# A state-space scan and an attention layer in one pipeline: TensorE's order made over two ticks, running sums on VectorE

## What is computed

```python
# layer 0, per image, over L = 4096 positions, 128 inner channels, 16 states
x, z = split(seq @ in_proj_w)
x = silu(conv1d(x, conv1d_w) + conv1d_b)             # 4 taps
dt, B, C = split(x @ x_proj_w)
delta = softplus(dt @ dt_proj_w + dt_proj_b)
h[t] = exp(delta[t] * A) * h[t-1] + (delta[t] * x[t]) * B[t]
y[t] = sum_n h[t] * C[t] + x[t] * D
seq = (y * silu(z)) @ out_proj_w
# layer 1, per image, hw = 4096
out_c = softmax(xc @ xc.T) @ x                       # 64 x 64
energy = q.T @ k                                     # 4096 x 4096
out_s = v @ softmax(energy, axis=-1).T
out = x + w_bn @ concat(out_c, out_s)
```

## Time and profile before

| | before |
|---|---|
| median of 3 runs | 8331.68 us (8329.12 to 8335.33) |
| profiled execution, span | 8332.7 us |
| PE busy | 7638.9 us, 92% |
| DVE busy | 6757.6 us, 81% |
| ACT busy | 5962.3 us, 72% |
| POOL busy | 3408.2 us, 41% |
| largest groups of PE | PV 2192.6 us, dif and max 1588.4 us, S 1567.9 and 1561.7 us, SUM 1071.1 us |
| largest groups of DVE | scan 2293.8 + 312.4 us, DBU 1514.0 us, maximum 1369.6 us |

### The profile page before, as it was taken

One profiled execution on the slowest core, in us unless ns is written; L12 is line 12 of the kernel. 1 busy time (PEld: TensorE's weight loads), 2 busy tenths in 40 slices (PEclk: granted clock), 3 DMA queues, 4 the chain that ended last, 5 costly groups with the idle time before them and its releaser, 6 DMA issues.

```text
span 8332.7 us, 153459 instructions
## 1 busy us (share of the span) xinstructions
PE 7638.9 (92%) x48454; PEld 2320.1 (28%) x48454; DVE 6757.6 (81%) x10982; ACT 5962.3 (72%) x10582; POOL 3408.2 (41%) x4135
## 2 busy tenths in 40 slices
PE   9963489999999999999989999999999999999999
PEld 2311122222222222222222222222222222222322
DVE  2238899898989898998989898998989898989721
ACT  1124578787877787887878787887877787878754
POOL 0016544444444444444444444444444444444300
PEclk9975699999999999999999999999999999999999
DMA  9838877878787878788777878787878878777500
GB/s 153 134 95 216 216 198 199 200 196 203 197 198 198 200 196 203 194 200 204 193 192 191 204 197 200 198 201 196 202 196 200 201 192 207 194 200 200 149 24 11
DMA packets 886525, 1531.01 MB, mean 184 GB/s; under 512 B 409480, under 2 KB 459472, under 8 KB 885712
## 3 DMA queue, kind: packets, MB, share of 16 engines
q1 hardware_dynamic: 882640, 1520.79, 74.8%
q10 hardware_dynamic: 3072, 0.40, 0.0%
HBM read 1326.69 MB, written 176.95 MB: 180 GB/s over the span
## 4 chain that ended last, share of the span: by engine, by line
PE 42%; ACT 3%; issue 2%; DMA 1%; ACTq 1%; DVE 1%; SPq 0%; DVEq 0%
PE bank L915 12%; PE bank L840 6%; PE bank L930 6%; PE bank L903 5%; PE bank L905 5%; PE bank L877 3%; ACT L1011 1%; ACT gains L956 1%; PE bank L885 1%; PE bank L872 1%; PE bank L862 1%; ACT pr L1011 1%; PE bank L858 1%; ACTq L1033 1%; DMA s1kx<-kx_d 1%
## 5 line engine op out<-in xcount | busy, mean ns | idle before, releaser
L1273 POOL TENSOR_TENSOR hst<-hst,cbc 128x512 f32<-128x512 f32 x2048 | 2609.9, 1274 | 3617.7 <-DVE bank L1145 3595.2
L1156 DVE TENSOR_TENSOR_SCAN hst<-dA,carry,bank 128x512 f32<-128x512 f32 x1792 | 2293.8, 1280 | 95.7 <-ACT dA L1017 23.7
L1011 ACT ACTIVATE pr<-bank 128x512 f32<-128x512 f32 x4096 | 2226.7, 603 | 59.4 <-PE bank L905 57.7
L915 PE MATMUL bank<-pr,vt 128*32 128x512 f32 x16384 | 2192.6, 607 | 0.0
L956 ACT ACTIVATE gains<-bank 128x512 f32<-128x512 f32 x2048 | 1224.2, 598 | 1106.1 <-PE bank L840 707.2
L1017 ACT ACTIVATE dA<-lanes,small 128x512 f32<-128x512 f32 x2048 | 1502.1, 733 | 349.8 <-DMA lanes<-spread_d 307.5
L840 PE MATMUL bank<-s1kx,s1q 128*128 128x512 bf16 x4096 | 1588.4, 389 | 160.8 <-DMA s1kx<-kx_d 84.4
L903 PE MATMUL bank<-s1q,s1k 128*128 128x512 bf16 x4096 | 1567.9, 383 | 175.0 <-ACT pr L1011 152.4
L1097 DVE CUSTOM_DVE_ANT_0 gains<-bank,gains 128x512 f32<-128x512 f32 x2048 | 1369.6, 669 | 328.9 <-PE bank L840 321.5
L1145 DVE TENSOR_TENSOR bank<-lanes,bbc 128x512 f32<-128x512 f32 x2048 | 1514.0, 739 | 116.9 <-DMA lanes<-spread_d 50.0
L905 PE MATMUL bank<-t2q,t2k 128*128 128x512 bf16 x4096 | 1561.7, 381 | 0.0
(11 more groups left out here) (116 smaller groups left out, 5705.3 us busy)
## 6 DMA issues: line engine op xcount, KB each, us to landing
lanes<-spread_d SPq DMA_DIRECT2D x2048, 512.0 KB, 5.9
seqt<-seq_d SPq DMA_DIRECT2D x256, 128.0 KB, 4.6
spread_d<-dsp SPq DMA_DIRECT2D x128, 256.0 KB, 2.0
spread_d<-usp SPq DMA_DIRECT2D x128, 256.0 KB, 2.0
bbc<-bc_d SPq DMA_DIRECT2D x128, 256.0 KB, 3.6
cbc<-bc_d SPq DMA_DIRECT2D x128, 256.0 KB, 4.2
xpad<-in_x SPq DMA_DIRECT2D x64, 256.0 KB, 6.7
ypad<-ypad SPq DMA_DIRECT2D x128, 128.0 KB, 4.1
```

The costliest lines, as they stand in the source:

```text
L915: mm = nc.tensor.matmul(ACC[CH * h + o:CH * h + o + BLOCK, :], vt[:, t, o:o + BLOCK], pr[:, T % PRING, h, :], start=t == 0, stop=t == KT - ...
L1011: nc.scalar.activation(pr[:, T % PRING, h, :], bank_of(("S", T, h))[:], ACT.Exp).then_inc(S["p_full"], 1)
L1156: nc.vector.tensor_tensor_scan(hst[:, slot_of(T), :], dA[:, T % 2, :], DBU[:], carry[:, g:g + 1] if sl % CHUNKS else 0.0, ALU.mult, ALU.ad ...
L1273: nc.gpsimd.tensor_tensor(h, h, cbc[:, (T - 1) // GROUPS % 2, :], ALU.mult).then_inc(S["hc_in"], 1)
```

## The change

TensorE's order is now written for two ticks at once: `plan` returns nothing for an odd T, and for an even T it issues `dif`, both halves of `S` and `max` of T and then of T + 1 (12 bf16 products in a row), then PV of T - 2 and of T - 1, then SUM, then the small products of both ticks together (`late_uses`). ACT and DVE take the small products of both ticks at the odd one. The steps that hang on them move by a tick: `y` is issued at r = 1 instead of 2, `BC` at 8 instead of 10, the first tap on ACT at r = 1 instead of 0, the taps 1 and 2 on DVE both at r = 2, `Abs` and `Exp` of the softplus on ACT at r = 7 instead of 6, `Ln` at 9 instead of 8, `dsp` on DVE and `usp` on POOL at 10 instead of 9, the stores of both at 11 instead of 10, `st_vt` at 14 instead of 13. `turn`, and with it the three small DMAs that bring the negated maximum to the queries, comes two ticks later (`TURN`). DVE takes the maximum between `DBU` and the scan instead of behind the scan. `ysb` signals a semaphore of its own, `y_took`.

Behind the last scan (`gathers`) SUM is left out: DVE adds the exponentials of every second tick into two running sums, kept in the buffers `lanes` that the scans no longer use, and one product group with ones (`TOTAL`) in a quarter sums them.

```diff
-TURN = SEARCH + KT + 1
+TURN = SEARCH + KT + 3
...
-                signal = {"S": "p_full"}.get(e[0], "dve_took" if e[0] in DVE_USES else "act_took")
+                signal = {"S": "p_full", "y": "y_took"}.get(e[0], "dve_took" if e[0] in DVE_USES else "act_took")
...
+    def gathers(self, T):
+
+        return not self.scans(T) and T >= 0 and self.attends(T) is not None
...
-        for name in {0: ("xin", "z"), 6: ("dt",), 10: ("BC",)}.get(r, ()):
+        for name in {0: ("xin", "z"), 6: ("dt",), 8: ("BC",)}.get(r, ()):
             if self.chunk(sl + 1):
                 ev.append((name, sl + 1))
-        name = {2: "y", 7: "out", 12: "xv", 14: "en"}.get(r)
+        name = {1: "y", 7: "out", 12: "xv", 14: "en"}.get(r)
         if name and self.chunk(sl - 1):
             ev.append((name, sl - 1))
         return ev
...
+    def late_uses(self, T):
+
+        return [e for e in self.small_uses(T) if e[0] not in ("dif", "max")]
+
     def plan(self, T):
-        uses = self.small_uses(T)
-        plan = [e for e in uses if e[0] == "dif"]
-        if self.attends(T):
-            plan += [("S", T, 0), ("S", T, 1)]
-        plan += [e for e in uses if e[0] == "max"]
+        if T % 2:
+            return []
+        plan = []
+        for t in (T, T + 1):
+            uses = self.small_uses(t)
+            plan += [e for e in uses if e[0] == "dif"]
+            if self.attends(t):
+                plan += [("S", t, 0), ("S", t, 1)]
+            plan += [e for e in uses if e[0] == "max"]
         if self.attends(T - 1):
-            plan.append(("PV", T - 1))
-        if T % 2 == 0 and self.attends(T - 1):
-            plan.append(("SUM", T // 2 - 1))
-        return plan + [e for e in uses if e[0] not in ("dif", "max")]
-
-
-SIGNAL_OF = {"PV": "pv", "SUM": "den"}
+            plan += [("PV", T - 2), ("PV", T - 1)]
+            if not self.gathers(T - 1):
+                plan.append(("SUM", T // 2 - 1))
+        if self.gathers(T - 2) and (T - 1 - MAIN) % KT == KT - 1:
+            plan.append(("TOTAL", T - 1))
+        return plan + self.late_uses(T) + self.late_uses(T + 1)
+
+
+SIGNAL_OF = {"PV": "pv", "SUM": "den", "TOTAL": "total"}
...
                     sched.note("da_in", T + 1)
                 if sched.fetches(T) is not None:
                     sched.note(f"lanes{sched.fetches(T) % SLOTS}", sched.fetches(T))
+                if sched.gathers(T - 1) and (T - 1 - MAIN) % KT >= 2:
+                    sched.note("gathered", T - 1)
                 if sched.scans(T - 1):
...
                         if sched.attends(T):
                             wait(act, "pv", (T - PRING,))
                             wait(act, "den", ((T - PRING) // 2,))
+                            wait(act, "gathered", T - PRING)
+                            if (T - MAIN) % KT in (PRING, PRING + 1):
+                                wait(act, "gathered", T - PRING + 2)
...
                             g = group_of(T + 1)
                             nc.scalar.activation(dA[:, (T + 1) % 2, :], lanes[:, (T + 1) % SLOTS, 0, :], ACT.Exp,
                                                  scale=amat[:, g:g + 1]).then_inc(S["da_in"], 1)
-                        for e in sched.small_uses(T)[len(near):]:
-                            small_use(e)
+                        if T % 2:
+                            for e in sched.late_uses(T - 1) + sched.late_uses(T):
+                                small_use(e)
...
                         done = sched.ended(T - 1)
                         if done:
                             wait(act, "st_den", sched.before(done), 16)
                             wait(act, "den", ((T - 1) // 2 - 1,))
+                            wait(act, "total", (T - 2,))
                             taken(act, ("res", sched.before(done)))
                             nc.scalar.copy(dens[:], DEN[:]).then_inc(S["den_in"], 1)
...
                             for s in range(3):
                                 act.dma_start(t2q[CH + s:CH + s + 1, q, :], nm3[:, s, :]).then_inc(S["nm_row"], 16)
                         c = sl + 1
...
                             nc.scalar.activation(em[:], dtx[:], ACT.Abs).then_inc(S["abs_in"], 1)
                             wait(act, "abs_in", c)
                             nc.scalar.activation(em[:], em[:], ACT.Exp, scale=-1.0).then_inc(S["em_in"], 1)
...
                             if due("em1_in", c):
                                 act.wait_ge(S["em1_in"], due("em1_in", c))
                             nc.scalar.activation(em1[:], em1[:], ACT.Ln).then_inc(S["ln_in"], 1)
...
-                                                           op0=ALU.mult, op1=ALU.add).then_inc(S["dve_took"], 1)
+                                                           op0=ALU.mult, op1=ALU.add).then_inc(S["y_took"], 1)
                         if sched.scans(T):
...
                             nc.vector.tensor_tensor(DBU[:], lanes[:, T % SLOTS, 1, :], bbc[:, sl % 2, :],
                                                     ALU.mult).then_inc(
                                 S["dbu_in"], 1)
+                        for e in ev:
+                            if e[0] == "max":
...
                             nc.vector.tensor_tensor_scan(
                                 hst[:, slot_of(T), :], dA[:, T % 2, :], DBU[:],
                                 carry[:, g:g + 1] if sl % CHUNKS else 0.0, ALU.mult, ALU.add).then_inc(S["scan"], 1)
-                        for e in ev:
-                            if e[0] == "max":
-                                small_use(e)
+                        T1 = T - 1
+                        if sched.gathers(T1) and (T1 - MAIN) % KT >= 2:
+                            quarter, t = sched.attends(T1), (T1 - MAIN) % KT
+                            into = gathered(quarter, t % 2)
+                            taken(dve, ("S", T1, 1))
+                            if t < 4:
+                                wait(dve, "total", (T1 - t - KT - 1,))
+                                taken(dve, ("S", T1 - 2, 1))
+                                before = pr[:, (T1 - 2) % PRING, :, :]
+                            else:
+                                wait(dve, "gathered", T1 - 2)
+                                before = into
...
                             if r == 0 and c % CHUNKS == 0:
                                 wait(dve, "conv", c - 2)
                                 nc.vector.memset(xin[:, 0, 0:D_CONV - 1], 0.0).then_inc(S["xin_in"], 1)
-                            if r == 1:
+                            if r == 2:
                                 wait(dve, "xin_in", c)
                                 taken(dve, ("xin", c))
                                 wait(dve, "gated", c - 1)
                                 wait(dve, "tap_in", c)
-                            if 1 <= r < D_CONV:
+                            for tap in {2: (1, 2), 3: (3,)}.get(r, ()):
                                 ins = nc.vector.scalar_tensor_tensor(
-                                    out=cacc[:], in0=x_[:, r:r + CHUNK], scalar=taps[:, r:r + 1], in1=cacc[:],
-                                    op0=ALU.mult, op1=ALU.add)
-                                if r < D_CONV - 1:
+                                    out=cacc[:], in0=x_[:, tap:tap + CHUNK], scalar=taps[:, tap:tap + 1],
...
                         if done:
                             wait(dve, "ld_rin", done, 32)
                             link(nc.vector.tensor_tensor(accs[:], accs[:], rinv[:], ALU.mult))
-                        for e in ev:
-                            if e[0] != "max":
-                                small_use(e)
+                        if T % 2:
+                            for e in sched.late_uses(T - 1) + sched.late_uses(T):
+                                if e[0] != "y":
+                                    small_use(e)
```

47 lines of the change are left out of this document (33 added, 14 removed).

## The result

The changed kernel takes 9300.4 us (median of 4 runs, 9296.6 to 9308.1) where the kernel before takes 8330.4 us in the same comparison: a ratio of 1.116, 95% interval 1.115 to 1.118, or 970 us slower. The forecast was 9080 us. Direction, range and the first mechanism came out. The size did not: 220 us are missing, and 9300 us lies above the forecast's own 8960 to 9200. The second fall of the clock, rival 2, which I had held for less likely, came true on top of the forecast.

What follows compares the result with a forecast made beforehand. TensorE sets the pace, VectorE 3 us behind per chunk. Per chunk -1.4 - 3.2 + 4.3 + 3.6 + 1.3 + 0.4 = +5.0 us, +7.0 with the clock; 118 chunks +826, tail -82: 9080 us (own range 8960 to 9200; wider range 8650 to 9330).

Steps and rivals of the forecast that it cites:

- the first mechanism: At the `dif` of r = 3, TensorE waits for `ysb` to free the bank of `y`: 4.3 us in each chunk.
- rival 2: Clock also falls at r = 10 and 11 behind two close idle pieces: another 2 us a chunk, 9310 us; chance 0.15.
- changes of form and old waits gone: TensorE in a chunk: seven fewer changes between bf16 and narrow products, -1.4 us; all old waits gone, -3.2 us.
- `y` ahead of the burst: At r = 3, `dif` waits while DVE does maximum, scan, two taps and `ysb`: 4.3 us lost in each chunk.
- clock at the y gap: TensorE idle 4.2 us at `y` makes the granted clock fall: chunk loss rises from +5.0 to +7.0 us.
- `Ln`, `BC`, `head` in one row: ACT's row with two table loads delays the exponentials; TensorE waits at r = 11, 3.6 us lost in each chunk.
- clock behind the Ln row: Second clock fall, at r = 10 and 11: nothing in the forecast's sum, another 2 us a chunk in rival 2.
- `Abs`, `Exp` behind `out`: At r = 7 ACT copies `out` first, so the `max` of r = 9 comes late: TensorE loses 1.3 us.
- small ones, `turn` among them: Later `turn` DMAs (0 or 1 us in every second chunk) and slightly late ACT: 0.4 us taken in a chunk.
- The tail: Behind the last scan, SUM and changes of form drop out, DVE's sums hide: -82 us.
- step 4: Sign in the changed kernel's profile: a wait for `pr` at r = 9, from `Abs` and `Exp` behind `out`.
- The maximum ahead of the scan costs nothing: DVE in each tick: same instructions, and `DBU` and scan need each other in either order; no cost taken.

Runs made afterwards that it cites:

- e2: Changed kernel with 16 idle bf16 products on TensorE ahead of the `dif` of r = 3, in the wait for `ysb`: 9148.2 us, ratio 1.098.
- b5: Changed kernel with 16 idle products in the wait at `y`, 10 behind the copy of `BC`, and `turn` two ticks earlier: 8814.1 us, ratio 1.058.
- e6: Changed kernel with ten idle bf16 products ahead of the `dif` of r = 11, once ACT has copied `BC`: 9255.8 us, ratio 1.110.
- b4: Changed kernel with `ysb` at r = 2, `Ln` at r = 8, `turn` two ticks earlier and VectorE's maximum behind the scan: 8720.6 us, ratio 1.046.
- e4: Changed kernel with `turn` two ticks earlier, as in the kernel before: 9156.9 us, ratio 1.099.
- e3: Changed kernel with ACT's `Ln` a tick earlier, at r = 8 instead of r = 9: 9427.6 us, ratio 1.131.
- b1: Changed kernel with three edits: `ysb` at r = 2, `Ln` at r = 8, `turn` two ticks earlier: 8498.0 us, ratio 1.020.
- e7: Changed kernel with VectorE's maximum behind the scan again, as before the change: 9034.8 us, ratio 1.084.
- b2: Kernel before, with the whole change only in the ticks behind the last scan: 8253.2 us, ratio 0.990.
- e1: Changed kernel with `ysb` formed a tick earlier, at r = 2 instead of r = 3: 8742.4 us, ratio 1.049.

## Why the prediction was right in sign and short in size

By its own steps, per chunk, forecast against measured (the ledger gives each):

| step | forecast | measured | from |
|---|---|---|---|
| changes of form and old waits gone | -4.6 | -5.89 | 51.66 - 57.55 |
| `y` ahead of the burst | +4.3 | +4.36 | 11.63 - 5.41, less the clock |
| clock at the y gap | +2.0 | +1.86 | e2 (b5: 1.79) |
| `Ln`, `BC`, `head` in one row | +3.6 | +3.95 | e6: 9.36 - 5.41 |
| clock behind the Ln row | 0, rival 2: +2 | +1.56 | e6 (b5: 1.46) |
| `Abs`, `Exp` behind `out` | +1.3 | +1.08 | 6.83 - 5.75 |
| small ones, `turn` among them | +0.4 | +1.87 | 1.10 + 0.63 + 0.14 |
| sum | +7.0 | +8.79 | 66.34 - 57.55 |

**What held.** The two big waits, the rows of VectorE and ACT that make them and their sizes, to 0.1 and 0.4 us. Counting on VectorE from the moment at which its first input exists gave the start of the `dif` of r = 3 to 0.03 us. The clock at `y` held too: one row of before, a gap of 4.13 us and what followed it, was enough to price it. The tail was forecast at -82 and measured at -81. Against the kernel before, 118 x 8.8 - 81 is 957 us of the 970; the 13 us left lie in the chunks at the ends, which the ledger leaves out.

**Right in size, wrong in place.** At `Ln` the prediction let the second half of S of r = 11 wait for the first exponential and the `max` for the second. The trace has the first half of S waiting 2.24 us for the ReLU, and the second half 1.30 us for the first exponential. At r = 9 it is the first half of S that waits, 0.92 us for the ReLU, and not the `max` for `pr`; the sign that I had named for step 4, a wait for `pr` at r = 9, did not show. In a ring of five the ReLU's bank comes round before those of the exponentials. As all of them stand in one row on ACT, the sums came out nearly the same.

**What failed, step by step.** The sum left out the second fall of the clock: "by this row the fall is seen only behind idle times of over 4 us". That sentence is true of the trace of before and was a wrong ground for 0.15, because that trace had no idle times of 2.2 and 1.3 us close together at all. No case seen is not a case against. The sentence also fails for single idle times: behind waits of 1.7 to 2.5 us at r = 0 the clock fell in 12 chunks of the changed kernel. The Trainium skill's section named there, "A second HAM failure mode: psum-queue depth-cycling" in "TensorE: Matmul & The Clock Gate", describes TensorE idling shortly between groups of products and paying for the clock again and again. Behind the rows of 5066.81 to 5070.00 this case's trace agrees, at 0.50, in each of the 116 chunks. Its price is 1.6 us in each chunk, about 185 us.

"The maximum ahead of the scan costs nothing: the same instructions" failed as a sentence, though not as a term. The scan's 1.28 us were in the y row's sum of 4.2 us, since I took the order as it stood; what I missed is that the move itself had put them there. It has a price of 2.3 us in a chunk with the wait for `y`, and is worth 1.9 without (b4). Counting instructions doesn't show that; what each of them needs does. The scan could run in VectorE's idle time and the maximum could not.

The small ones were mis-sized: 0.4 forecast, 1.9 measured. `turn` is 1.2 of it by e4, at (0,1) and (12,13). The upper bound that I gave for it, 1 us in every second chunk, was too low: the waits are 1.4 us on average and up to 2.5, with 4.8 us from the last of the three issues to the score that waits. Behind 12 of them the clock fell, at 1.5 us each. For the remaining 0.7 no run stands.

Against these, the old waits and forms gave 1.3 us more than I let go. The wait for the keys, 84.4 us before and 11.2 after, is 0.6 of a chunk and was in my 2.3 us; which part of the rest is form and which is wait no experiment separates. That rival 2's sum, 9310 us, ends 10 us from the result is therefore luck: its clock term was 0.4 us too high, the small ones 1.5 and the Ln row 0.35 too low, and the gain 1.3 too small.

## What to carry to other kernels

When an order is made coarser, follow each buffer that used to be freed inside the old, finer unit: price the wait from the moment at which the freeing engine's first input exists, through everything it has queued, and ask which of those instructions could have run in the idle time ahead of it. A mend tested alone can show little, or a loss, when a DMA that is issued no earlier, a new or longer fall of the clock or waits behind it take its gain back (e2, e3, e6); test it together with what it uncovers (b1, b5), and expect a small reordering to change its sign with its surroundings (e7, b4). And where a change has a good part in one stretch and a bad one in another, confine it: b2 keeps the 81 us and pays nothing for them.

## What the runs showed of the hardware

The granted clock fell in each of 116 chunks behind two idle times of 2.24 and 1.30 us, with two bf16 products between them, although neither is long; with ten idle products in place of the first it did not fall behind the 1.30 us that stayed (e6, b5). Behind two idle times of about 1.3 and 1.08 us at r = 10 and 11, with a few products between them, it never fell (e3, b1). A single idle time of the size of the first can be enough: at r = 0 of the changed kernel it fell behind 12 of 56 waits of 0.73 to 2.52 us, none of the 12 shorter than 1.70, with TensorE busy for the 6 us ahead of them. In e3 it fell behind all 56 waits of 2.16 to 4.05 us there, many of them with another idle time shortly ahead; in e6 29 waits of 1.48 to 3.01 us brought no fall and 27 of 1.96 to 3.19 us did. Behind the y gap's 4.20 us it fell each time, behind 3.03 us in 72 chunks of 116 (e7). So between 1.7 and 3.0 us the length of the idle time alone does not decide it, and these runs don't show what does.

A fall costs 1.5 to 1.9 us wherever its price could be read: 1.86 at `y` (e2), 1.68 there in e7, 1.56 behind the Ln row (e6), 1.5 to 1.7 at r = 0.

The two falls of a chunk aren't independent. With the fall at `y` gone, by idle products (e2) or by no wait (e1), the stretch at 0.50 behind the Ln row starts earlier and lasts 6.6 and 6.7 us on average instead of 3.5, and costs another 0.9 us. Why the earlier stretch had shortened the later one is open; the rows show only that it did.
